# One graph network, two mixtures of experts: attention's edge records leave from a ring of 32 groups spread over three stages, and both expert stages are rewritten

## What is computed

```
x = x + gnn0(layernorm(x), src, dst, edge_weight)         # h = x W_l; segment_sum(w * h[src]) + x W_r + biases
x = x + ffn0(layernorm(x))                                # 8 experts 256 -> 1024 -> 256, relu, best one only
x = x + gnn1(layernorm(x), edge_index, edge_attr_16)      # attention, 4 heads of 64, 50,000 edges + self loops
x = x + ffn1(layernorm(x))                                # 8 experts 256 -> 512 -> 256, gelu, best two
...
# ffn0: the capacity is ceil(1.25 * T / 8) places for each expert
pos = (cumsum(one_hot, axis=0) * one_hot).sum(-1) - 1     # place of a token in its expert's buffer
kept = pos < C                                            # tokens beyond the capacity get 0
buf = zeros((E, C, D)).at[idx, pos_safe].set(x, mode='drop')
hmid = relu(einsum('ecd,edf->ecf', buf, w1) + b1)
ybuf = einsum('ecf,efd->ecd', hmid, w2) + b2
y = nan_to_num(ybuf[idx, pos_g] * (prb * kept), posinf=1e4, neginf=-1e4)
# ffn1: cw holds the two largest probabilities of each token, 0 elsewhere
out = sum over experts of cw[:, e] * (gelu(xf @ W1[e] + b1[e]) @ W2[e] + b2[e])
```

## Time and profile before

| what | value |
|---|---|
| median of three executions | 3166.48 us (3164.11 to 3168.03) |
| profiled execution, and its span | 3162.6 us, 3160.9 us |
| mean granted TensorE clock | 0.796 |
| busy: PE, DVE, POOL, ACT | 2312.0 (73%), 2183.7 (69%), 1523.6 (48%), 1066.1 us (34%) |
| prepare, convolve | 0 to 306, 306 to 913 us |
| experts_top1 | 914 to 1493 us |
| attend_prepare, attend, attend_finish | 1493 to 1593, 1593 to 2595, 2597 to 2702 us |
| experts_top2 | 2703 to 3161 us |

### The profile page before, as it was taken

One profiled execution on the slowest core, in us unless ns is written; L12 is line 12 of the kernel. 1 busy time (PEld: TensorE's weight loads), 2 busy tenths in 40 slices (PEclk: granted clock), 3 DMA queues, 4 the chain that ended last, 5 costly groups with the idle time before them and its releaser, 6 DMA issues. The chain is left out here.

```text
span 3160.9 us, 60071 instructions
## 1 busy us (share of the span) xinstructions
PE 2312.0 (73%) x15090; PEld 1721.7 (54%) x15091; DVE 2183.7 (69%) x8253; ACT 1066.1 (34%) x3566; POOL 1523.6 (48%) x1506
## 2 busy tenths in 40 slices
PE   2786667787754899600879999999999982609990
PEld 0664333333334555400569999999999971506660
DVE  9996677666653211143779999999999989434453
ACT  1000100000000222100458888888888871201110
POOL 0223777777767777776044444444444410060006
PEclk6787776655555899855989999999999985559995
DMA  5401333533451334111333333333333332422214
GB/s 179 146 20 22 90 91 98 146 102 98 102 77 49 106 123 118 34 52 30 114 90 75 72 74 75 75 74 73 75 75 74 73 69 85 146 80 63 63 56 129
DMA packets 272960, 268.21 MB, mean 85 GB/s; under 512 B 147403, under 2 KB 228999, under 8 KB 272289
## 3 DMA queue, kind: packets, MB, share of 16 engines
q0 software_dynamic: 63616, 145.86, 17.7%
q1 hardware_dynamic: 204322, 114.71, 13.0%
q10 hardware_dynamic: 4736, 4.29, 0.4%
HBM read 196.38 MB, written 68.34 MB: 84 GB/s over the span
## 5 line engine op out<-in xcount | busy, mean ns | idle before, releaser
L1639 POOL DMA_INDIRECT l_rows<-xl_tab,l_ra x440 | 463.8, 1054 | 497.6 <-DMA l_ra<-rec_a 393.9
L790 PE MATMUL c_ps<-c_rows,c_hot 128*128 128x256 f32 x864 | 433.9, 612 | 176.3 <-DVE c_hot L917 78.2
L772 POOL DMA_INDIRECT c_rows<-h_tab,c_rec x432 | 454.0, 1051 | 144.4 <-issue 96.3
L1033 POOL DMA_INDIRECT rec_a<-m_stage_r,m_stage_i x390 | 385.9, 990 | 118.9 <-issue 116.5
L790 PEld LDWEIGHTS c_ps<-c_rows,c_hot 128*128 128x128 f32 x864 | 194.9, 277 | 414.8 <-DVE c_hot L917 256.1
L1783 DVE CUSTOM_DVE_ANT_0 l_junk<-l_ps_lb,l_pen 128x256 bf16<-128x256 f32 x880 | 319.4, 420 | 5.9 <-PE l_ps_lb L1745 4.4
L924 DVE TENSOR_TENSOR x_sb<-x_sb,c_ps 128x256 f32 x432 | 181.6, 420 | 190.7 <-PE c_ps L790 177.7
L1702 PE MATMUL l_bank_l<-g_att_d,l_rz 128*128 128x4 f32 x1760 | 238.3, 256 | 4.0 <-ACT l_rz L1689 1.6
L1677 ACT ACTIVATE l_val<-l_rows,l_val 128x64 f32<-128x64 f32 x880 | 234.2, 337 | 7.1
L1667 ACT ACTIVATE g_acc<-g_acc,l_cexp x880 | 234.0, 345 | 1.1 <-issue 0.9
L1702 PEld LDWEIGHTS l_bank_l<-g_att_d,l_rz 128*128 128x128 f32 x1760 | 219.3, 191 | 20.9 <-ACT l_rz L1689 6.1
(11 more groups left out here) (478 smaller groups left out, 5704.4 us busy)
## 6 DMA issues: line engine op xcount, KB each, us to landing
m_w<-in_L_ffn_w SPq DMA_DIRECT2D x16, 1024.0 KB, 9.2
rec_a<-p_blank SPq DMA_DIRECT2D x110, 102.0 KB, 2.4
l_ra<-rec_a SPq DMA_DIRECT2D x220, 51.0 KB, 2.1
e_w<-in_L_ffn_W SPq DMA_DIRECT2D x16, 512.0 KB, 9.7
xd_buf<-attr_mid SPq DMA_DIRECT2D x7, 1024.0 KB, 11.5
e_xin<-xd_buf SPq DMA_DIRECT2D x56, 128.0 KB, 2.1
ye_buf<-e_yout SPq DMA_DIRECT2D x56, 128.0 KB, 1.7
l_rows<-xl_tab,l_ra POOLq DMA_INDIRECT x440, 3.0
```

The lines of the kernel that those rows point to most:

```text
L772: pool.indirect_dma_start(rows[:, u, :], None, K["h_tab"], bass.IndirectOffsetOnAxis(ap=rec[:, n % RSLOTS, k, 0:1].bitcast(I32), axis=0)). ...
L790: pe.matmul(ps[s % NB][:, :], hot[:, u, :], rows[:, u, :], start=True, stop=True).then_inc(s_agg, 1)
L1033: pool.indirect_dma_start(K["rec_a"], bass.IndirectOffsetOnAxis(ap=stage_i[:, u, k:k + 1], axis=0), stage_r[:, u, k, :], None).then_inc(s_ ...
L1639: pool.indirect_dma_start(rows[:, u, j, :], None, K["xl_tab"], bass.IndirectOffsetOnAxis(ap=ra[:, u, j, A_SRC:A_SRC + 1].bitcast(I32), axi ...
```

## The change

**A ring for attention's records.** The staging slots become 32, in one SBUF room (`room_a`) that other stages use at other times. `convolve` stages the tail and 8 groups on DVE between its last blocks, and POOL scatters the tail and 3 groups at its end. `experts_top1` scatters 5 groups, sends, scatters 39 groups, and gathers. `attend_prepare` scatters the last 31 groups and waits for all.

**Top-1 stage.** Tiles go through the node step in quads with the gate as the stationary operand (8 x 512 scores, bias added by DVE, transposed back). The next expert's transposes stand behind the hidden layer of this one. The output bias is one bfloat16 matmul with three rows (`b2_rows`) and opens the sum. The results are awaited five tiles at a time and multiplied by ACT; DVE has two operations per chunk fewer, and the statistics for attention are taken chunk by chunk.

**Top-2 stage.** Quads as well. Normalised tiles are stored by ACT into `xn_tab`. Nothing is sent: 50 float32 matmuls of one-hot tiles (`hot_p`, `hot_t`) yield, for each of the 56 x 128 places, which token it holds (`found`). POOL gathers each input tile (`from_i`) and scatters each output tile to the token's own rows (`to_i`), so the results come back in five plain DMAs of SP. The shares are computed behind the tables, and the tile loop is written out without a loop.

```diff
+RING = 32
+IN_CONV = 3
+FIRST_SCAT = 8
+BEFORE_GOT = 47
+BEFORE_ATT = 47
+QUAD = 4
+U_SEND = 8
...
+def scatter_group(pool, K, g):
+    u = g % RING
+    pool.wait_ge(K["s_staged"], g + 2)
+    pool.nop(nofuse=True)
+    for k in range(GRP):
+        pool.indirect_dma_start(K["rec_a"], bass.IndirectOffsetOnAxis(ap=K["stage_i"][:, u, k:k + 1], axis=0),
+                                K["stage_r"][:, u, k, :], None).then_inc(K["s_scat_a"][u], 16)
...
# convolve, POOL
+            scatter_tail(pool, K)
+            for g in range(IN_CONV):
+                scatter_group(pool, K, g)
...
# convolve, DVE, in the loop over blocks
+                if 401 <= s < 401 + 2 * FIRST_SCAT and s % 2:
+                    stage_group(dve, K, (s - 401) // 2)
...
# experts_top1, POOL
+            scatter(range(IN_CONV, FIRST_SCAT))
+            for s in range(NT):
...
+                pool.indirect_dma_start(K["xd_buf"], bass.IndirectOffsetOnAxis(ap=to_i[:, s % U:s % U + 1], axis=0),
+                                        xn[:, s % U, :], None).then_inc(s_sent[s % U], 16)
+            scatter(range(FIRST_SCAT, BEFORE_GOT))
             pool.wait_ge(s_from, 1)
...
-                                        ).then_inc(s_got[0], 16)
-            for u in range(U_SCAT):
-                scatter(LAST * U_SCAT + u, u, LAST, None)
-            for u in range(U_SCAT):
-                pool.wait_ge(s_scat[u], 16 * (GRP * GROUPS // U_SCAT + (1 if u == 0 else 0)))
+                                        ).then_inc(s_got[tile // CT], 16)
+            scatter(range(BEFORE_GOT, BEFORE_ATT))
...
# experts_top1, PE
+                    for k in range(2):
+                        mm = pe.matmul(ps_y[v % 2][0:EXP0, 0:n], gate[:, k, :], xt[:, v % 2, k, 0:n],
+                                       start=(k == 0), stop=(k == 1))
...
+                if s + 1 < EXP0:
+                    inputs(s + 1)
                 pe.wait_ge(s_hc, NF * s + NF)
...
+                    pe.matmul(ps_y[q % 2][:, 0:D], K["ones_b"][0:3, :], b2_rows[:, s, :], start=True, stop=False)
...
# experts_top1, ACT and DVE on the results
+                act.activation(got[:, tile, :], got[:, tile, :], ACT.Copy, scale=den[:, tile:tile + 1]
+                               ).then_inc(s_val, 1)
...
-            dve.wait_ge(s_got[0], 16 * NT)
-                o.did(dve.tensor_tensor(y3, y3, den[:, t0:t0 + CT].rearrange("p (t o) -> p t o", o=1)
-                                        .to_broadcast([P, CT, D]), ALU.mult))
+                dve.wait_ge(s_val, 1 + t0 + CT)
-                o.did(dve.tensor_scalar(ok, y, BIGF, None, ALU.is_le))
+                o.did(dve.tensor_scalar(ok, y, 0.0, 0.0, ALU.mult, ALU.is_equal))
-                o.did(dve.scalar_tensor_tensor(out=ok, in0=y, scalar=-BIGF, in1=ok, op0=ALU.is_ge, op1=ALU.mult))
+                for s in range(t0, t0 + CT):
+                    o.did(dve.bn_stats(stats[:, s, :], x[:, s, :]))
...
# attend_prepare, POOL, behind the memsets
+            for g in range(BEFORE_ATT, GROUPS):
+                scatter_group(pool, K, g)
+            for u in range(RING):
+                pool.wait_ge(K["s_scat_a"][u], 16 * (GRP * len(range(u, GROUPS, RING)) + (1 if u == 0 else 0)))
...
# experts_top2, PE: which token stands at which place
+            for g in range(NB):
+                pe.wait_ge(s_onehot, g + 1)
+                for k in range(2 * CT):
+                    mm = pe.matmul(ps_found, hot_p[:, g % 2, k, :], hot_t[:, g % 2, k, :],
+                                   start=(g == 0 and k == 0), stop=(g == NB - 1 and k == 2 * CT - 1))
+                mm.then_inc(s_code, 1)
...
# experts_top2, POOL
+            pool.wait_ge(s_from, 2)
+            pool.wait_ge(s_xnst, 16 * len(QUADS))
+            LAG = XR + 4
+            for s in range(NTOP2 + LAG):
+                if s < NTOP2:
+                    wait(pool, s_xp, s - XR + 1)
+                    pool.indirect_dma_start(xin[:, s % XR, :], None, K["xn_tab"],
...
+                if s >= LAG:
+                    r = s - LAG
+                    pool.wait_ge(s_yc, r + 1)
+                    pool.indirect_dma_start(K["ye_buf"], bass.IndirectOffsetOnAxis(ap=to_i[:, r:r + 1], axis=0),
...
# experts_top2, SP: the results
+            for g in range(NB):
+                t0, t1 = g * CT, min(g * CT + CT, NT - 1)
+                sp.dma_start(results(g)[:, 0:t1 - t0, :, :],
+                             y_rows[t0 * P:t1 * P, :, :].rearrange("(t p) k d -> p t k d", p=P)).then_inc(s_got[g], 16)
```

More of the change, by code:

```diff
@@ L14 @@
+import math
 from contextlib import ExitStack
@@ L1077, in _, with inputs @@
             act.wait_ge(s_b1, 1)
-            act.activation(b1t[:, :], ps_t[:, 0, 0:EXP0 * NF], ACT.Copy).then_inc(s_b1t, 1)
-            def expert(s, u, i, _):
+            act.activation(b1t[:, :], ps_y[0][:, 0:EXP0 * NF], ACT.Copy).then_inc(s_b1t, 1)
+            act.wait_ge(s_b1t, 1)
+            def inputs(s):
                 for k in range(2):
@@ L1084, in expert @@
                     act.activation(xint[:, k, :], ps_x[:, k, :], ACT.Copy).then_inc(s_xc, 1)
+            inputs(0)
+            for s in range(EXP0):
+                u = s % 2
                 wait(act, s_yp, NQ * s)
@@ L1102, in _ @@
             pe.wait_ge(s_small, 64)
-            def node(s, u, i, _):
-                if live(s, 0, NT):
-                    pe.wait_ge(s_xn, s + 1)
-                    wait(pe, s_xtc, s - 1)
+            for g in range(len(QUADS) + 3):
+                if g < len(QUADS):
+                    quad = QUADS[g]
+                    pe.wait_ge(s_xn, quad[-1] + 1)
+                    wait(pe, s_xtc, 2 * g - 2)
                     for k in range(2):
-                        mm = pe.transpose(ps_xn[u][:, k, :], xn[:, u, k * P:(k + 1) * P], ident[:, :])
+                        for j, tile in enumerate(quad):
+                            mm = pe.transpose(ps_xn[g % 2][k][:, j * P:(j + 1) * P], xn[:, tile % U, k * P:(k + 1) * P],
+                                              ident[:, :])
@@ L2042, in experts_top2 @@
-        s_xin = [sem(f"e_xin{k}") for k in range(UT)]
-        s_yst = [sem(f"e_yst{k}") for k in range(4)]
-        s_xp, s_xc, s_hp, s_hb, s_g, s_tp, s_tc, s_yp, s_yc, s_from, s_one, s_sum, s_out = (
-            sem("e_" + n) for n in ("xp", "xc", "hp", "hb", "g", "tp", "tc", "yp", "yc", "from", "one", "sum", "out"))
-        GT = 5
-        first, second = (ps[:, 0:2 * P].rearrange("p (k n) -> p k n", k=2) for ps in ps_h)
-        ps_xn = [(ps_t, first, ps_t, first, second)[k] for k in range(U)]
+        s_small, s_const, s_dve, s_var, s_std, s_xn, s_xt, s_xtc, s_lp, s_lt, s_back = (
+            sem("e_" + n) for n in ("small", "const", "dve", "var", "std", "xn", "xt", "xtc", "lp", "lt", "back"))
@@ new lines, in experts_top2 @@
+        s_shift, s_exp, s_hot, s_rank, s_lg = (sem("e_" + n) for n in ("shift", "exp", "hot", "rank", "lg"))
+        s_w, s_tab, s_xnst, s_onehot, s_code, s_found, s_from = (
+            sem("e_" + n) for n in ("w", "tab", "xnst", "onehot", "code", "found", "from"))
+        s_xin = K["dma_sems"]("e_xin", XR)
+        s_yst = K["dma_sems"]("e_yst", YR)
+        s_got = [sem(f"e_got{k}") for k in range(NB)]
+        s_xp, s_xc, s_hp, s_hb, s_g, s_tp, s_tc, s_yp, s_yc, s_one, s_sum, s_out = (
+            sem("e_" + n) for n in ("xp", "xc", "hp", "hb", "g", "tp", "tc", "yp", "yc", "one", "sum", "out"))
@@ L2057, in experts_of, with results @@
-            return before
-        def expert_of(ctx, u, r):
-            return ctx[UT + u - r]
+            return packed(nc, tab[0:1, :], NTOP2, BITS_E, PACK_E, engine, EXP1 - 1)
+        def results(g):
+            return got[0][:, g * CT:(g + 1) * CT] if g < 3 else got[1][:, (g - 3) * CT:(g - 2) * CT]
         @block.sync
@@ L2150, in _ @@
             pe.wait_ge(s_small, 32)
-            def node(s, u, i, _):
-                if live(s, 0, NT):
-                    pe.wait_ge(s_xn, s + 1)
-                    wait(pe, s_xtc, s - 1)
+            for g in range(len(QUADS) + 3):
+                if g < len(QUADS):
+                    quad = QUADS[g]
+                    pe.wait_ge(s_xn, quad[-1] + 1)
+                    wait(pe, s_xtc, 2 * g - 2)
                     for k in range(2):
-                        mm = pe.transpose(ps_xn[u][:, k, :], xn[:, u, k * P:(k + 1) * P], ident[:, :])
+                        for j, tile in enumerate(quad):
+                            mm = pe.transpose(ps_xn[g % 2][k][:, j * P:(j + 1) * P], xn[:, tile, k * P:(k + 1) * P],
+                                              ident[:, :])
@@ L2355, in _ @@
-            o.then()
-            dve.scalar_tensor_tensor(out=tab[:, 1:], in0=b[:, :, 1], scalar=float(1 << BITS_E), in1=b[:, :, 0],
-                                     op0=ALU.mult, op1=ALU.add).then_inc(s_tab, 1)
             dve.wait_ge(s_tab, 1)
+            experts = experts_of(ENG.DVE)
             dve.wait_ge(s_w, 16 * (2 * EXP1 + 2))
-            def tile(s, u, i, ctx):
```

(15 more changed lines are left out.)

743 lines of the change are left out of this document (390 added, 353 removed).

## The result

The changed kernel takes **3000.3 us** (median of four runs, 2998.7 to 3002.6) against 3166.1 us for the kernel before on the same chip: ratio 0.948, 95% interval 0.9468 to 0.9491. The forecast was 3022.5. The profiled execution has a span of 2999.1 us, to be set against 3160.9.

A forecast was written before the change was run, and what follows sets the result against it. Bounds differ by stage, with POOL paying 1.26 us per indirect DMA. Terms: -53 until attend starts, -91 in top-2, sum -144; 3018.6 + 3.9 gives 3022.5 us. Sum's own range 3000 to 3050, whole range 2992 to 3065.

The forecast's parts named there:

- Convolve's end: End of convolve: 16 scatters take 20.2 us, to 919.0, so the top-1 stage starts at 920.3, +6 us.
- Node steps: Quads in both expert stages: between 22 us at full clock and 44 at half; 35 taken, top-2 gaining 15.
- rival (4): More is won: quads and one-hots reach full clock in both stages, some 2992 us; chance 0.10.
- a clock in the quads that is not 0.50: Sign for the node steps: the prediction is wrong if PE's clock there differs from 0.50.
- First send: Top-1 stage: start, statistics, node steps and ranking put POOL's first send at 976.5 against 999.4 us.
- Experts: Top-1 experts: 30.4 us each instead of 34.2, two waits of 1.95 us gone; 250 us in all, end at 1265.
- POOL's 195 scatters: Beside the top-1 experts: 246 us from the last send, to 1254, hidden with 11 us to spare.
- Results: End of top-1: first gather at 1271, first chunk 1282, DVE's chunks 44 us, stage end 1328 instead of 1493.
- attend_prepare: Stage bound by POOL's 155 scatters: 211 us, to 1540, with 6 us for a busy DVE; attend starts 53 us earlier.
- Rival (1): In attend_prepare DVE's operations and POOL's generation of 155 scatters exclude each other: 3082 us; chance 0.08.
- Top-2: Top-2 stage: node steps -15, shares -2, last place to first product -40, loop unchanged, behind the loop -34; together -91 us.
- Rivals (2) and (3): Top-2 loop: POOL's gather-scatter pair at 5.1 us gives 3078 (chance 0.08); at 6.7 or more, 3166 and more (0.03).

The follow-up runs named there:

- gate8: Changed kernel with node steps one tile at a time, the tile stationary, eight gate columns moving and bias added by DVE: 3022.9 us (0.9528 to 0.956 of before).

## Why the prediction was right, and where it was off

**Convolve's end**: forecast +6, measured +11.9 for the start of top-1. The 16 scatters took 20.2 us as said (901.0 to 921.3). The rest: POOL's last gather ended 2.2 us later (1.1 of it came from `prepare`), and from the last scatter's end to the next stage there were 4.7 us, where I had 1.3. That is the first of two places where POOL's drain was left out.

**Node steps**: the term that was mis-sized. I took 35 us a stage, nearer to the price at half clock (44) than to that at full clock (22); measured 21.9 and 20.9, at full clock after two quads. This is the first part of rival (4), which had a chance of 0.10, and one of the prediction's own signs of being wrong, a clock in the quads that is not 0.50. The ground for the choice was that the stretch had stood at 0.50 before although PE was busy; gate8 shows that this hung on the form with the tile stationary, which the quads give up. The other part of rival (4) did not come: the one-hot products ran at 0.50, as the sum had them. First send 972.2 instead of 976.5, although the stage started 5.6 us later than forecast: 10 us better. In top-2 the places were done 28 us earlier relative to the stage's start, for 17 forecast.

**Experts**: 247.3 us (1010.3 to 1257.6) for 250; the cycle and both waits as forecast. Inputs landed in 4.2 to 13.4 us and held PE up by less than 1 us behind the first expert. **POOL's 195 scatters** ended 10.7 us ahead of the first gather: less to spare than forecast, since the forecast's 11 us are counted to PE's last product, and to that it was 6.6 us (1251.0 to 1257.6).

**Results**: first gather 4 us behind the last product for 6 forecast, first chunk 10 us after it for 11; DVE's chunks 45 us for 44. ACT and POOL stayed behind DVE, though gathers went out 1.62 us apart in the mean, held by DVE's operations as found above.

**attend_prepare**: 218.5 us for 212. Scatters beside the stage's own work were 1.30 us apart, the others 1.265, so contention cost 2 us and not 6. Rival (1) did not happen, though the hold that it rests on is real: it adds up all of DVE's busy time, while the runs above show that a scatter waits for the rest of the operation that it meets and gets on behind it. DVE's operations in this stage are short (0.69 us at most), which I take for the reason why the rest is small, without a run that shows it in this stage. What was missing is POOL's drain: 13.8 us between the last scatter and the next stage, where I had a landing and a start. That is the second place.

**Top-2**: place to first product -39.6 for -40 (21.6 us of products for 21), the loop -1.1 for 0, behind the loop -37.8 for -34 (the first load was there after 9.0 us with the last scatter's landing in it, for 10.8 forecast, and an addition took 0.46 us for 0.50). Rivals (2) and (3) did not happen: PE's busy time in the loop is as before.

So the mechanism of each part was right but for the clock in the quads and POOL's drain. The 22 us are the node steps (10 and 11 us), small terms, and 4 us from setting the forecast 3.9 us above the profiled execution, an addition that the changed kernel's runs do not show (profiled 3000.9, median 3000.3); less convolve's end (5.6) and `attend_prepare` (6.5). That these have opposite signs is luck, and without it the time would have lain some 34 us below the forecast, under the 3000 of the narrower range. The chances add up to 1.07, since the half of (4) that the range takes in stands in both.

## What to carry to other kernels

Indirect DMAs of one engine had one price here, 1.26 us, for rows of 204 as of 1024 bytes, so place them by counting the free microseconds of that engine stage by stage. Spread until it is idle nowhere that others wait, and no further: in top-1 the next stage started 11.2 to 11.6 us behind POOL's last DMA wherever it waited for POOL. Look at what DVE does beside them: an indirect DMA waits for the end of the DVE operation that it meets, so long operations without gaps are the dear neighbours. A float32 product of one row for a bias took about as long as one of 128 x 128 (0.59 us for two records, 0.69 for two); fold it into another engine's copy. Before blaming the clock for a slow stretch, count instructions: the half-clock form with six records tied with a full-clock form of seven.
